# A second buffer for the turned sums and for their two parts, an eighth pair of exponentials, and a new table of order, in a six-layer attention kernel

## What is computed

```python
q = split_heads(x @ Wq.T + bq); k = split_heads(ctx @ Wk.T + bk); v = split_heads(ctx @ Wv.T + bv)
scores = einsum('bqhd,bkhd->bhqk', q, k) / sqrt(16)      # 16 heads
probs = softmax(where(mask, scores, min))                # SELF: causal mask instead
h = einsum('bqhk,bkhd->bqhd', probs, v).reshape(B, Q, 256) @ Wo.T + bo
y = layer_norm(h + x) * ln_g + ln_b                      # FFN: x + relu(ln(x) @ w1 + b1) @ w2 + b2
```

## Time and profile before

| | us |
|---|---|
| median of 3 runs (1275.99 to 1277.92) | 1276.8 |
| the profiled execution, its own time | 1274.86 |
| its span (first to last instruction) | 1273.1 |
| PE busy | 1211.0 (95%) |
| DVE busy | 1041.7 (82%) |
| ACT busy | 789.8 (62%) |
| POOL busy | 747.4 (59%) |

### The profile page before, as it was taken

The page is one execution under the profiler, slowest core; times in us unless marked ns, Lnnn a source line. Parts: engine busy times, 40 slices in busy tenths (PEclk is TensorE's granted clock), DMA queues, the critical chain, the costliest instruction groups (busy, mean ns, idle before and its releaser), DMA issues.

```text
span 1273.1 us, 41776 instructions
## 1 busy us (share of the span) xinstructions
PE 1211.0 (95%) x18188; PEld 977.8 (77%) x18188; DVE 1041.7 (82%) x1749; ACT 789.8 (62%) x1225; POOL 747.4 (59%) x879
## 2 busy tenths in 40 slices
...
GB/s 239 120 51 21 17 34 18 18 34 10 30 27 2 10 3 2 19 27 2 3 2 3 10 18 11 50 11 43 1 11 7 1 1 25 10 11 9 59 11 84
DMA packets 16077, 33.87 MB, mean 27 GB/s; under 512 B 2039, under 2 KB 6423, under 8 KB 15895
## 3 DMA queue, kind: packets, MB, share of 16 engines
...
...
## 4 chain that ended last, share of the span: by engine, by line
PE 60%; DVE 26%; POOL 5%; issue 4%; ACT 4%; DMA 1%; POOLq 0%; SPq 0%; DVEq 0%; ACTq 0%
DVE s_nm L1546 10%; PE ps L1224 7%; PE ps L1239 7%; PE ps L1193 6%; PE ps L1212 6%; PE ps L1156 6%; PE ps L1094 5%; PE ps L1041 5%; PE ps L1053 4%; DVE s_KH L1500 4%; PE ps L1066 3%; DVE s_Os L1553 3%; ACT s_PU L1390 2%; PE ps L1114 2%; PE ps L1030 2%
## 5 line engine op out<-in xcount | busy, mean ns | idle before, releaser
L1546 DVE TENSOR_REDUCE s_nm<-ps 128x8 fp32r<-128x960 f32 (+1 forms) x352 | 397.6, 1162 | 54.2 <-PE ps L1094 29.2
L1390 ACT ACTIVATE s_PU<-ps 120x1024 f32<-120x1024 f32 (+1 forms) x288 | 281.0, 1025 | 117.1 <-PE ps L1171 116.5
L1156 PE MATMUL ps<-s_Qs,s_KH 32*120 32x256 f32 (+2 forms) x4608 | 191.8, 288 | 13.8 <-DVE s_Os L1553 5.3
L1156 PEld LDWEIGHTS ps<-s_Qs,s_KH 32*120 32x120 f32 (+1 forms) x4608 | 155.1, 179 | 42.6 <-issue 16.9
L1742 POOL TENSOR_TENSOR s_Os<-s_Os,s_Rc 128x512 f32<-128x512 f32 x80 | 87.9, 1099 | 161.9 <-DVE s_Rc L1561 156.0
L1193 PE MATMUL ps<-s_PU,s_Vp 120*32 120x256 f32 x2048 | 135.1, 385 | 7.4 <-DVE s_nm L1546 4.3
L1094 PE MATMUL ps<-s_KH,s_Qs 32*128 32x240 f32 x3072 | 128.5, 292 | 8.3 <-DVE s_nm L1546 3.0
L1681 POOL TENSOR_TENSOR s_xs<-s_xs,s_rowv 128x512 f32<-128x512 f32 x96 | 126.2, 1314 | 12.3 <-ACT s_nt L1286 1.2
L1212 PE MATMUL ps<-s_W,s_oT 128*128 128x256 f32 x896 | 126.2, 289 | 5.9 <-POOL s_oT L1702 3.6
L1702 POOL TENSOR_TENSOR s_oT<-s_On,s_oT 128x512 fp32r<-128x512 f32 x48 | 62.6, 1305 | 114.0 <-ACT s_oT L1399 112.6
L1094 PEld LDWEIGHTS ps<-s_KH,s_Qs 32*128 32x128 f32 x3072 | 103.4, 187 | 30.1 <-issue 9.3
...
## 6 DMA issues: line engine op xcount, KB each, us to landing
...
s_mi<-mask SPq DMA_DIRECT2D x8, 3.8 KB
...
```

Source lines behind the costliest of these rows:

```text
L1156: t = e.matmul(banks[j][0:n, wide * x:wide * x + wide], kz[row[j], lk, g, c, k0:k0 + n], q[row[j], lq, g, qs_], start=(x == 0 and y_ == 0) ...
L1390: t = e.activation(P_of(i, k)[0:n, :, :], pair("B", i, k)[0:n, :, :], ACT.Exp, scale=0.25)
L1546: e.tensor_reduce(o, v, AX.X, ALU.max, negate=True).then_inc(sem["max"])
```

## The change

On and oT get a second buffer, PU an eighth. 1,024 bytes are asked for as the scratch of dynamic DMAs, in place of the default, which makes room in SBUF. The kernel's code is otherwise the same; every row of the table of numbers is new (one is shown), and with it the order on all five lists.

```diff
-    ("K", "SELF"): (381.06, 406.91, 423.63, ...
+    ("K", "SELF"): (379.62, 405.22, 416.48, ...
...
-        self.ring = {"Q": Slots(4), "KH": Slots(2), "K0": Slots(1), "PU": Slots(7), "Vp": Slots(2), "cT": Slots(2),
-                     ... "On": Slots(1), "oT": Slots(1), "nm": Slots(2), "mT": Slots(2),
+        self.ring = {"Q": Slots(4), "KH": Slots(2), "K0": Slots(1), "PU": Slots(8), "Vp": Slots(2), "cT": Slots(2),
+                     ... "On": Slots(2), "oT": Slots(2), "nm": Slots(2), "mT": Slots(2),
...
-        PU = [sb(f"PU{i}", [128, 2, 512]) for i in range(7)]
+        PU = [sb(f"PU{i}", [128, 2, 512]) for i in range(8)]
...
-        On = [sb(f"On{i}", [128, 2, S]) for i in range(1)]
-        oT = [sb(f"oT{i}", [128, 2, 2, S], f32r) for i in range(1)]
+        On = [sb(f"On{i}", [128, 2, S]) for i in range(2)]
+        oT = [sb(f"oT{i}", [128, 2, 2, S], f32r) for i in range(2)]
...
-    nc = bacc.Bacc("TRN2", target_bir_lowering=False, num_devices=1)
+    nc = bacc.Bacc("TRN2", target_bir_lowering=False, num_devices=1, dynamic_dma_scratch_size=1024)
```

More of the change, by code:

```diff
@@ L172 @@
-    ("cap", "SELF"): (424.56, 439.42, 460.13, 477.56, 490.39, 509.34, 532.46, 544.5, 563.09, 587.99, 603.02, 618.58, 640.51, 665.96, 678.67, 697.63, 413.11, 435.64,
[8 rows of a table removed]
-    ("rec", "SELF"): (436.18, 452.63, 473.01, 488.01, 507.72, 526.53, 543.25, 571.74, 584.04, 601.4, 621.15, 644.24, 657.23, 674.84, 698.5, 713.26),
-    ("nmul", "SELF"): (438.2, 453.03, 474.54, 488.41, 508.12, 530.48, 550.59, 572.14, 591.49, 601.8, 629.83, 645.05, 657.63, 677.45, 699.84, 713.66),
-    ("turn", "SELF"): (439.39, 456.93, 477.48, 489.86, 509.31, 532.98, 559.8, 573.33, 595.53, 611.8, 635.26, 658.61, 670.71, 679.21, 702.83, 716.17),
@@ L184 @@
-    ("OTh", "SELF"): (442.07, 458.74, 479.54, 491.41, 510.25, 533.81, 564.74, 576.96, 597.19, 612.63, 641.62, 659.44, 671.98, 680.04, 704.44, 718.04),
-    ("OTl", "SELF"): (442.76, 459.43, 480.23, 499.43, 511.08, 540.03, 565.43, 584.29, 601.65, 617.86, 644.49, 660.13, 675.09, 684.98, 710.62, 719.68),
[29 rows of a table removed]
-    ("max", "CROSS"): (701.76, 706.67, 724.46, 734.42, 742.8, 759.52, 770.23, 781.81, 792.72, 804.17, 816.59, 829.78, 844.88, 853.23, 864.91, 881.83, 703.51, 704.61,
-        725.53, 733.35, 741.11, 758.46, 771.29, 780.75, 794.41, 805.24, 818.84, 828.71, 845.95, 852.16, 866.23, 880.77, 708.8, 711.42, 731.76, 744.44, 750.71, 764.06,
-        776.6, 783.14, 801.32, 807.87, 822.38, 837.67, 848.59, 858.9, 875.5, 884.37, 707.73, 713.51, 728.16, 745.76, 749.65, 765.13, 777.67, 784.86, 800.25, 808.93,
-        824.03, 836.6, 849.65, 859.97, 873.76, 885.44),
@@ L234 @@
-    ("nmul", "CROSS"): (728.04, 745.91, 753.88, 773.34, 782.23, 796.16, 807.99, 819.56, 825.49, 844.6, 851.12, 868.09, 880.4, 894.52, 906.65, 941.09),
-    ("turn", "CROSS"): (731.08, 747.54, 755.07, 775.76, 786.52, 802.38, 811.6, 821.7, 831.44, 847.91, 858.03, 869.28, 882.9, 898.24, 920.61, 942.28),
-    ("OTh", "CROSS"): (734.66, 749.48, 758.28, 780.14, 788, 803.21, 812.43, 822.53, 835.04, 848.74, 862.77, 874.33, 890.63, 902.46, 928.87, 943.11),
-    ("OTl", "CROSS"): (736.09, 750.3, 758.97, 780.83, 788.69, 803.9, 814.91, 824.03, 835.73, 849.43, 863.46, 875.02, 891.32, 913.93, 929.56, 943.8),
[88 rows of a table removed]
[126 rows of a table added]
@@ new lines @@
+    ("rec", "SELF"): (431.82, 449.22, 471.96, 486.18, 503.97, 523.25, 539.97, 560.65, 595.99, 600.66, 616.46, 636.36, 652.42, 671.22, 692.64, 706.54),
+    ("nmul", "SELF"): (432.22, 449.62, 472.36, 486.58, 504.37, 527.2, 547.31, 561.81, 596.39, 601.06, 623.53, 636.76, 652.82, 672.04, 693.04, 706.94),
+    ("turn", "SELF"): (433.41, 456.32, 474.27, 488.81, 505.82, 529.7, 556.52, 571.9, 597.58, 607.78, 635.68, 647, 656.84, 673.23, 695.42, 708.13),
+    ("OTh", "SELF"): (434.24, 457.99, 475.43, 492.55, 506.65, 530.53, 558.82, 573.54, 598.76, 610.83, 636.81, 648.46, 662.07, 678.45, 699.06, 708.96),
@@ new lines @@
+    ("OTl", "SELF"): (437.28, 458.86, 477.61, 493.24, 508.99, 536.75, 561.83, 579.01, 599.86, 612.72, 638.35, 656.04, 669.65, 679.14, 705.74, 712.73),
[29 rows of a table added]
+    ("max", "CROSS"): (697.45, 699.23, 720.15, 727.97, 737.41, 753.3, 768.07, 774.8, 787.66, 798.38, 810.71, 824.14, 839.02, 848.51, 858.96, 875.88, 696.38, 701.29,
+        719.08, 729.03, 735.73, 754.37, 764.86, 775.86, 788.73, 799.44, 811.78, 823.07, 840.08, 846.83, 860.95, 874.81, 704.04, 710.07, 722.77, 741.09, 745.33, 758.59,
+        770.7, 777.36, 794.46, 803.05, 817.12, 831.27, 843.68, 852.95, 868.14, 878.42, 702.35, 706.79, 725.45, 739.06, 744.27, 759.66, 772.02, 778.42, 795.52, 801.99,
+        816.05, 832.33, 842.62, 854.69, 869.83, 879.48),
@@ new lines @@
+    ("M", "CROSS"): (705.35, 716.68, 728.56, 742.6, 748.03, 763.98, 774.5, 781.56, 798.97, 804.66, 820.14, 833.76, 845.12, 857.36, 873.41, 880.7),
+    ("mTe", "CROSS"): (706.06, 717.21, 729.29, 743.83, 749.11, 764.69, 775.43, 785.33, 799.93, 805.24, 821.37, 834.28, 846.52, 858.31, 873.94, 881.76),
[4 rows of a table added]
+    ("exp", "CROSS"): (712.23, 720.41, 732, 745.81, 758.3, 769.37, 781.31, 792.89, 804.33, 812.04, 826.11, 836.29, 851.38, 860.29, 876.06, 882.86, 710.19, 721.32, 733.39,
[7 rows of a table added]
+    ("rec", "CROSS"): (722.26, 740.84, 747.48, 763.99, 771.77, 787.41, 790.99, 812.84, 813.89, 833.4, 851.82, 858.28, 874.25, 882.1, 908.47, 915.58),
```

21 lines of the change are left out of this document (11 added, 10 removed), and 592 rows, old and new, of tables (AT, WANT).

## The result

The changed kernel takes 1262.1 us (median of 4 executions, 1261.8 to 1265.1) against 1277.2 for the kernel before beside it: 0.9892 of before, 95% interval 0.9878 to 0.9905, that is 13.8 us less by the ratio and 15.1 by the medians. I had forecast 1268.3 and a range from 1264.0 to 1275.5. Faster was right; it was faster than the range allows.

What follows compares the result with a forecast made beforehand. PE was taken as the bound, busy 1211.0 of 1273.1 us, held up mostly by DVE until 720 us. Terms -0.9 - 3.4 - 2.8 - 1.3 + 0.5 - 0.6 = -8.5 us gave 1268.3 us on the median's scale, range 1264.0 to 1275.5.

Steps and rivals of the forecast that it cites:

- Buffers alone 0: Second On and oT and eighth PU without the new order remove no wait of the trace: 0 us.
- The end -2.8: Last items: O and PV move behind item 95's D, and the last O runs at full clock: -2.8 us.
- The wait at the border -0.9: Border to CROSS: item 45's statistics leave DVE's path to L1500, so PE's 2.09 us wait falls to 1.2: -0.9 us.
- Place 3 +0.5: Item 40: D comes directly behind M, so PE idles until mTe is there, where PV covered it: +0.5 us.
- The signs for the profile: Expected if right: PE idle near 56 us, L1500 waits about 2.5, no half clock at the border, last O 1.2 us.
- four other waits on L1500: -1.3: PE's waits for the rest of the keys at items 10, 14, 34, 35, 2.6 us in all, half won: -1.3 us.
- Rival B: Up to 720 us DVE sets the pace, so only the end gains: -2.8 us, 1274.0 us; chance 0.16.
- The clock behind the border -3.4: Behind the border to CROSS, 6.8 us at half clock vanish because PE's wait before is shorter: -3.4 us.
- Rival A: The clock falls all the same at the border to CROSS, so 3.4 us stay: -5.1 us, 1271.7 us; chance 0.18.
- D's mechanism: PE's many small waits for maxima (L1546) in L0, L1 and L3 shrink too: 6 us more, 1262 us; chance 0.08.
- Rival C: POOL blocks DVE's L1500 more often; delay up by a third costs 13.7 us, giving 1282 us; chance 0.10.
- tiling, -0.6: PE's list has six fewer changes between row strips and columns, at most 1.1 us, half taken: -0.6 us.

Runs made afterwards that it cites:

- e13: Kernel before with the changed order from 1220 us to the end, two On, two oT, seven PU, and the changed list of outputs: 1273.2 us, 0.9980.
- e11: Kernel before with the changed order from 1220 us to the end, two On, two oT, seven PU, old list of outputs: 1275.6 us, 0.9995.
- e12: Kernel before with the changed order from 1220 us to the end, one On, two oT, seven PU, old list of outputs: 1276.1 us, 1.0008.
- e6: Kernel before with one DVE step moved: item 45's statistics stand behind the rest of item 48's keys (L1500): 1272.9 us, 0.9977.
- e2: Kernel before with the changed order in SELF's first half only, eight PU, one On, one oT: 1270.3 us, 0.9955.
- e3: Kernel before with the changed order in SELF's first half only, adapted to seven PU, one On, one oT: 1269.6 us, 0.9951.
- e19: Changed kernel, buffers kept, with the order of before in SELF's first half: 1270.8 us, 0.9966 of before.
- e9: Kernel before with only PE's list changed: second B and D of items 33, 34, 35 ahead of the next item's first A: 1279.4 us, 1.0027.
- e10: Kernel before with only DVE's list changed: six statistics steps in SELF's first half stand two to five steps later: 1281.6 us, 1.0040.

## Why the prediction was wrong, and where it was right

Right by its own steps:
- *Buffers alone 0*: 0.9996.
- *The end -2.8*: -2.6 alone (e13), with the last O at 1.22 us. That the size fits is partly luck. I priced the chain up to the last y; in before the span ends 8.6 us behind y of item 94, with ten outputs in a row, and the chain alone gains nothing (e11, 0.9995). The old outputs' list costs 1.9 us (e11 against e13); I had not read SP's list at all. Of the buffers I wrote that the second ones are needed, and gave a reason for oT alone; what the second On is worth (1.7 us, e12 against e11) is not clear of noise.
- *The wait at the border -0.9*: in e6 2.09 became 0.84, with the pair of L1500 at 2.58 us; in the changed kernel it became 0.31, with the pair at 2.05. My sum left the pair at 3.06. By the Trainium skill, "SBUF — State Buffer", "Who interferes with whom", I had estimated 2.5; the traces are at its side, not at my sum's.
- *Place 3 +0.5*: D of item 40 waits 0.47 for ACT's mTe.
- The signs for the profile: PE idle 54.8 us for 56 forecast, PE's waits on L1500 2.4 for 2.5.

Wrong:
- **The failed step is the price of the middle: the only term for it was "four other waits on L1500: -1.3", and PE's other waits there stood at nothing, with the reason that DVE's work is only moved and late elsewhere.** The waits on L1500 themselves gave 0.5 net. What the sum had at nothing was the bulk: SELF's first half gave 5.7 to 6.2 us alone (e2, e3) and 8.7 when taken out again (e19, 1.7 of them the wait where the orders meet). I priced the middle by the waits of one line, L1500, because the change's new order at these places was easiest to see there. These were 1.4 of 7.7 us in that stretch; bank waits behind X and Tl, and waits behind values and exponentials, were the greater part. DVE was busy 83% of the window around SELF, not saturated, so its lateness there could go by order. Rival B rested on the same reading and fell too.
- *The clock behind the border -3.4*: the mechanism was right, the size not. Half clock for 6.8 us cost 2.5 us and not 3.4, a fall came in nine of eleven executions with the long wait and in none of nine with the short one, and its mean cost is 1.6 us. In the profiles compared the stretch behind the border gave 2.0. The Trainium skill, "TensorE: Matmul & The Clock Gate", Part 1, says that the place of a change of clock varies between runs of one kernel. The eleven profiles, of kernels with one order at that place, agree, and I ought to have priced the term as a mean.
- *Scale*: I added 1.9 us for a profiled execution below the median of before. The changed kernel's profiled execution lies on its median, so 1.9 of the miss are this.
- Rival A did not come: no fall at the border. D's mechanism, shorter waits for maxima, gave little: PE's waits on L1546 are 16.0 us in all before and 15.0 after, 3.0 in 4 waits at L1094 in both. Rival C, the slowdown through POOL, went the other way. The group of L1500 in the changed kernel, against the earlier trace rows:

```profile
L1500 DVE SCALAR_TENSOR_TENSOR s_KH<-s_K,s_cst,s_KH 128x480 fp32r<-128x480 f32 (+1 forms) x96 | 85.9, 935 | 3.3 <-ACT s_KH L1366 3.2
```

10.8 us of DVE's time less, more than DVE's whole gain of 9.7. In e3 it is 94.3, so 2.4 of them belong to SELF's first half. What the other 8 are worth was not tried by itself; 4.5 of them lie between 32 and 240 us (the writes of s_KH by DVE there: 21.9 us before, 17.5 after), and that stretch is no faster.

In the traces the miss adds up: forecast -8.5, measured -12.7, so -4.2. A of 32 to A of 48 gave -7.6 for -1.1 (-6.5); A of 48 to A of 50 -2.0 for -3.4 (+1.4); up to A of 32 +0.4 for -0.6 (+1.0); from A of 50 on -3.5 for -2.8 (-0.7); tiling, -0.6, does not show (+0.6).

Open: which single moves inside SELF's first half carry the gain, and how much of it is the shorter pairs of L1500 there rather than PE's waits in a new order. e9 and e10 show only that these moves of PE's or DVE's alone don't carry it.
